# Swapped projections in place of the exchange between partitions, for the first half of the first head pair of each batch

## The reference

```python
q = (xn @ q_w + q_b).reshape(b, s, H, HD).transpose(0, 2, 1, 3)
k = (xn @ k_w + k_b).reshape(b, s, H, HD).transpose(0, 2, 1, 3)
v = (xn @ v_w + v_b).reshape(b, s, H, HD).transpose(0, 2, 1, 3)
# _rope(x): x1, x2 = x[..., 0::2], x[..., 1::2]
#   concatenate([x1 * cos - x2 * sin, x1 * sin + x2 * cos], axis=-1)
q, k = _rope(q, theta), _rope(k, theta)
scores = jnp.einsum('bhqd,bhkd->bhqk', q, k) * scale   # causal softmax follows
```

## Time and profile before

| | us |
|---|---|
| median of 3 runs (2248.17 to 2252.59) | 2251.11 |
| the profiled execution | 2248.88 |
| its span, first to last instruction | 2247.1 |
| TensorE busy | 1943.8 (87%) |
| VectorE busy | 1620.2 (72%) |
| ScalarE busy | 1459.2 (65%) |
| GpSimd busy | 948.8 (42%) |

### The profile page before, as it was taken

How to read it: one execution, slowest core, us unless ns; L and a number is a source line. 1 busy time by engine, 2 the same in 40 slices (tenths; PEclk the granted TensorE clock), 3 DMA queues, 4 the chain that set the end, 5 groups by cost and what they waited for, 6 DMA issues and landing times. The chain is left out here.

```text
span 2247.1 us, 33201 instructions
## 1 busy us (share of the span) xinstructions
PE 1943.8 (87%) x10218; PEld 1300.2 (58%) x10218; DVE 1620.2 (72%) x3001; ACT 1459.2 (65%) x2909; POOL 948.8 (42%) x909
## 2 busy tenths in 40 slices
PE   3759999889985999988988699998898679999798
PEld 1236676657524767665742567676574256676566
DVE  4867777658696777766768777775777877776587
ACT  2528777657652878765765477775675367777576
POOL 2555353234365443413436635341443564352243
PEclk9879999989987999998989799999998989999899
DMA  2001111001101111100110111110010011010011
GB/s 80 1 21 43 28 37 32 8 22 41 38 0 34 30 39 26 39 10 20 41 31 0 43 29 37 33 28 15 22 40 15 1 42 43 22 41 20 20 35 33
DMA packets 63328, 64.09 MB, mean 29 GB/s; under 512 B 12104, under 2 KB 46256, under 8 KB 63152
## 3 DMA queue, kind: packets, MB, share of 16 engines
q1 hardware_dynamic: 63152, 61.96, 10.5%
HBM read 26.26 MB, written 2.10 MB: 13 GB/s over the span
## 5 line engine op out<-in xcount | busy, mean ns | idle before, releaser
L787 ACT ACTIVATE probs<-ps,least 128x640 f32<-128x640 f32 (+7 forms) x512 | 380.6, 743 | 85.9 <-DVE least L1134 74.6
L799 ACT ACTIVATE probsT<-ps 128x512 f32<-128x512 f32 (+3 forms) x768 | 348.4, 491 | 120.3 <-PE ps L1504 111.9
L1504 PE MATMUL ps<-ident,probs 128*128 128x128 f32 x2304 | 349.2, 277 | 11.8 <-ACT probsT L799 4.5
L1494 PE MATMUL ps<-k_high,q_split 128*128 128x512 f32 (+3 forms) x768 | 303.6, 395 | 54.5 <-DVE q_split L1124 37.0
L1504 PEld LDWEIGHTS ps<-ident,probs 128*128 128x128 f32 x2304 | 271.3, 141 | 51.8 <-issue 22.6
L509 POOL TENSOR_SCALAR inverse_wide<-inverse 128x512 f32<-128x512 f32 x64 | 39.7, 621 | 545.8 <-DVE inverse L1145 545.8
L1141 DVE TENSOR_REDUCE least<-ps 128x1 f32<-128x640 f32 (+3 forms) x256 | 262.2, 1024 | 8.8
L1515 PE MATMUL ps<-probsT,vals 128*64 128x512 f32 (+3 forms) x1408 | 265.4, 498 | 0.4
L1495 PE MATMUL ps<-k_low,q_split 128*128 128x512 f32 (+3 forms) x768 | 261.5, 353 | 0.0
L1494 PEld LDWEIGHTS ps<-k_high,q_split 128*128 128x128 f32 x768 | 147.9, 193 | 177.6 <-ACT probs L787 85.7
L870 ACT ACTIVATE hid<-ps,cols 128x512 f32<-128x512 f32 x256 | 176.3, 689 | 112.6 <-PE ps L1341 112.2
(11 more groups left out here) (222 smaller groups left out, 3996.3 us busy)
## 6 DMA issues: line engine op xcount, KB each, us to landing
roped<-turned SPq DMA_DIRECT2D x512, 64.0 KB, 2.0
w<-in_w SPq DMA_DIRECT2D x128, 128.0 KB, 2.0
w_pair<-in_w_pairs SPq DMA_DIRECT2D x32, 128.0 KB, 2.6
xin<-in_x SPq DMA_DIRECT2D x4, 512.0 KB, 4.3
out<-acc SPq DMA_DIRECT2D x4, 512.0 KB, 3.2
pos<-in_c_pos SPq DMA_DIRECT2D x1, 512.0 KB, 4.7
v_w<-in_v_w SPq DMA_DIRECT2D x1, 512.0 KB
o_w<-in_o_w SPq DMA_DIRECT2D x1, 512.0 KB
```

The costliest lines, as they stand in the source:

```text
L787: act.activation(probs[:, t % 2, 0:width(t)], banks(2 * (t % 2))[:, 0:width(t)], ACT.Exp, bias=least[:, t:t + 1], scale=-1.0, accum_out=ro ...
L799: act.activation(dst, ps[:, T_BANK + g % 2, 0:k1 - k0], ACT.Copy).then_inc(t_taken, 1)
L1494: pe.matmul(o, q, k_high[par][h][:, k0:k1], start=True, stop=False)
L1504: made = pe.transpose(ps[:, T_BANK + g % 2, at - k0:at - k0 + P], probs[:, t % 2, at:at + P], ident[:, :])
```

## The change

For the first half of the first pair of each batch, the swapped sine part is computed and not fetched. A second weight tensor `w_sw` (columns in swapped order, one DMA at the start, split into high and low parts by GpSimd once) gives the projection with its partitions already exchanged, in banks 2 and 3. VectorE multiplies it by sin and subtracts it from the cosine part, in place of the exchange and GpSimd's addition. On GpSimd `acc` stands behind the preparation of both halves. On TensorE the values stand behind the scores of units 0 and 1, and on VectorE the order of the second half's products, the minima and the values changes. The second half and all other pairs keep the exchange.

```diff
@@ program: buffers, semaphores
+SW_BANK = (2, 3)
+        w_sw = sb("w_sw", [P, 2, P])
+        w_sw_high, w_sw_low = sb("w_sw_high", [P, 2, P], F32R), sb("w_sw_low", [P, 2, P], F32R)
...
@@ sync
+            sp.dma_start(w_sw[:, :, :], ins["w_pairs"][0:1, :, 1::2, :].rearrange("o p s n -> p (o s) n")).then_inc(w_sw_in, 16)
             part_end(sp, 1)
...
-                    for c in range(HALVES):
+                    for c in range(HALVES) if p else (1,):
@@ gpsimd, once, before the batches
+            pool.wait_ge(w_sw_in, 16)
+            pool_copy(pool, w_sw_high[:, :, :], w_sw[:, :, :]).then_inc(w_sw_split, 1)
+            pool.wait_ge(w_sw_split, 1)
+            pool.tensor_tensor(w_sw_low[:, :, :], w_sw[:, :, :], w_sw_high[:, :, :].bitcast(F32), ALU.subtract
+                               ).then_inc(w_sw_split, 1)
+            pool.wait_ge(w_sw_split, 2)
@@ gpsimd, prepare
                     def add(j):
-                        pool.wait_ge(swapped[j], DMA_ALL * (m + 1))
+                        if (p, c) == (0, 0):
+                            pool.wait_ge(roped_ready, 2 * m + j + 1 + 2)
+                            return
+                        pool.wait_ge(swapped[j], DMA_ALL * (m - b))
@@ gpsimd, each batch
                 pool.wait_ge(xn_split, 2 * b + 2)
+                for c in range(HALVES):
+                    prepare(0, 0, c, lambda k: k, lambda: None)
                 pool.wait_ge(y_stored, 16 * b + 16)
                 pool.wait_ge(tok_ready, 2 * b + 2)
                 steps.link(pool.tensor_tensor(acc[:, :, :], xa[:, :, :], gamma1_r.unsqueeze(1).broadcast_to((P, TILES, P)),
                                               ALU.mult))
                 pool.tensor_tensor(acc[:, :, :], acc[:, :, :], o_b_r.unsqueeze(1).broadcast_to((P, TILES, P)),
                                    ALU.add).then_inc(acc_ready, 1)
-                for c in range(HALVES):
-                    prepare(0, 0, c, lambda k: k, lambda: None)
@@ vector
-                for g in range(4):
-                    sine(b * PAIRS, 0, g, g, PROLOGUE_BANK[g])
-                    cosine(0, g, PROLOGUE_BANK[g])
+                for j in range(2):
+                    m = HALVES * b * PAIRS
+                    dve.wait_ge(x_out, X_ALL * b + j + 1)
+                    dve.wait_ge(roped_ready, 2 * m + j + 1)
+                    cosine(0, j, PROLOGUE_BANK[j])
+                    dve.wait_ge(sw_out, 2 * b + j + 1)
+                    dve.scalar_tensor_tensor(roped[:, j, cols_of(0)], ps[:, SW_BANK[j], :], cols[:, C_QK + 2 * (1 - j) + 1:
+                                             C_QK + 2 * (1 - j) + 2], sin_t[:, cols_of(0)], ALU.add, ALU.mult
+                                             ).then_inc(sine_ready, 1)
+                    dve.wait_ge(x_taken, X_ALL * b + j + 1)
+                    dve.wait_ge(sine_ready, 2 * m + j + 1)
+                    dve.sem_inc(passed, 1)
+                    dve.tensor_tensor(roped[:, j, cols_of(0)], turned[:, 0, j, :], roped[:, j, cols_of(0)], ALU.subtract
+                                      ).then_inc(roped_ready, 1)
+                sine(b * PAIRS, 0, 2, 2, PROLOGUE_BANK[2])
                 for h in range(2):
                     low(b * PAIRS, 0, 0, h)
+                sine(b * PAIRS, 0, 3, 3, PROLOGUE_BANK[3])
+                smallest(b * PAIRS, 0)
+                cosine(0, 2, PROLOGUE_BANK[2])
+                cosine(0, 3, PROLOGUE_BANK[3])
+                smallest(b * PAIRS, 1)
                 for c in range(2):
                     values(0, 0, 4 + c, c, PROLOGUE_BANK[c])
-                for t in range(2):
-                    smallest(b * PAIRS, t)
@@ tensor
                     project(g, 0, PROLOGUE_BANK[g])
+                    if g < 2:
+                        if (b, g) == (0, 0):
+                            pe.wait_ge(w_sw_split, 2)
+                        parts_product(ps[:, SW_BANK[g], :], w_sw_high[:, 1 - g, :], w_sw_low[:, 1 - g, :], cut(xn_high, 0),
+                                      cut(xn_low, 0), True, True).then_inc(sw_out, 1)
+                for t in range(2):
+                    scores(b * PAIRS, 0, t)
                 for c in range(2):
                     bank_free(c + 1)
                     values(0, c, PROLOGUE_BANK[c])
-                for t in range(2):
-                    scores(b * PAIRS, 0, t)
```

More of the change, by code:

```diff
@@ L326, in program @@
         w_pair_high_ready, w_pair_split = sem("w_pair_high_ready"), sem("w_pair_split")
+        w_sw_in, w_sw_split, sw_out = sem("w_sw_in"), sem("w_sw_split"), sem("sw_out")
         x_out, x_taken = sem("x_out"), sem("x_taken")
```

## The result

The changed kernel takes 2255.47 us in the median of 20 runs (2251.34 to 2260.53), the kernel before 2249.26 in 20 runs beside them. The ratio is 1.0028 with a 95% interval of 1.0018 to 1.0038: 6.3 us slower, 4.0 to 8.5. The profiled executions are nearer together: 2252.60 against 2248.88, spans 2250.8 against 2247.1. One execution of experiment 4, 3599 us at a lower clock, was disturbed and is left out of its ratio; all others are counted.

What follows compares the result with a forecast made beforehand. Bound: each batch's opening, a latency chain with GpSimd in it. Late third sine products, 3 x 0.5 + 1.0 = +2.5 us, on the profiled 2248.88 give 2251.4, median 2253.6, said as 2253.5; range 2244 to 2260.

Steps and rivals of the forecast that it cites:

- the gate: Pair 1's third sine product on VectorE waits for GpSimd's fifth addition: 0.5 us late, 1.0 in fourth batch, +2.5 in all.
- Keys, queries, low parts: Batch 0's opening: keys 152.5, queries 155.05, low parts 158.8, scores 159.0, first exponential 160.1, 5.4 us early.
- The mutual exclusion: Low parts: two-input operations of VectorE and GpSimd follow one another; mere sharing would make the sum about 4 us smaller.
- Values in the path: Values behind the first scores on TensorE put pair 1's projection at 163.55, leaving 1.8 of 5.4 us.
- rival B: All 5.4 us of the earlier first exponential stay, needing the values hidden too: 2229.5 us; chance 0.03.
- the alternative of the text: With the clock at its upper level from 163.5 on, GpSimd's fifth addition would end at about 174.5.
- My own case: The forecast sum with pair 1's third sine product late, +2.5 us; own range 2246.5 to 2257.6; chance 0.58.
- rival C: TensorE's clock low after VectorE's stall: +1.1 to +2.2 us per batch, +7 to +11 in all, about 2260; chance 0.20.
- the sign that the prediction set for C: Third sine product at 174.7, but the step ends over 1 us later, with granted clock 0.5 after the stall.
- C's last sentence: Decisive is whether the stall's gap at TensorE matches its idle stretch when the clock fell; stall computed near 3 us.
- A: GpSimd gets through `acc` sooner or VectorE arrives later, so the 1.8 us stay: -7.2 us, 2244; chance 0.13.
- D: VectorE's subtraction waits for GpSimd's copies, shrinking the head start by a further us; same time as forecast; no separate chance.

Runs made afterwards that it cites:

- experiment 4: Kernel before with only the `acc` operations moved late, behind GpSimd's part of the first step: 2248.98 us, ratio 1.0010.
- Experiment 6: Changed kernel with `acc` back at its old place, ahead of pair 0's preparation: 2251.12 us, ratio 1.0003 against the kernel before.
- experiment 1: Changed kernel with `acc` moved later still, behind GpSimd's part of the first step: 2243.23 us, ratio 0.9969 against the kernel before.
- experiment 3: Changed kernel with `acc` behind GpSimd's part of the first step and the values ahead of the first scores: 2239.64 us, ratio 0.9952 against the kernel before.
- experiment 2: Changed kernel with the values back ahead of the first scores on TensorE: 2253.83 us, ratio 1.0023 against the kernel before.
- experiment 7: Kernel before with only the `acc` operations moved behind pair 0's preparation: 2265.80 us, ratio 1.0075.
- experiment 5: Changed kernel with fifteen unread products on TensorE in each first step's stall: 2256.47 us, ratio 1.0028 against the kernel before.
- experiment 8: Experiment 5 with VectorE's first two low parts one unit later: 2251.22 us. Its line, from six kernels: rest of step is 20.74 to 20.77 plus unit 7's low part.

## Why the prediction was right, and where it wasn't

The forecast was 2253.5, the measurement 2255.47, inside the range, and part of that is luck. The forecast was +2.4 us on a median of 3 runs, 2251.11; 20 runs of the kernel before gave 2249.26, and the measured change is +6.3. Against the profiled execution, to which the sum was made, the forecast was +2.5 and the marks give +4.67, with the gate booked too high, the clock not at all, and a third term that nobody had (the holds, below). By its own steps, in batch 0's times:

*Keys, queries, low parts.* Keys 152.59 (forecast 152.5), queries 154.73 (155.05), low parts done 158.36 (158.8), scores 158.57 (159.0), first exponential 159.57 (160.1). The mutual exclusion on which the low parts' time rested is there: GpSimd's two operations take 2.93 us together, VectorE's two take 2.93 us as well, and they end 0.55 apart. Experiment 6 shows it by itself, a subtraction of 2.81 beside `acc` against 0.69. The Trainium skill (SBUF — State Buffer, "SBUF: two separate sides") says the same, as a lock held for the whole instruction, and the rows agree.

*Values in the path.* 163.46 against 163.55: of the first exponential's head start, the six takings leave 1.9 us. Experiments 1 and 3 show that this much is real and is kept where nothing downstream takes it: 2.20 earlier at pair 1's first sine product and 2.16 at the end of the step in experiment 1 (against before), 2.82 and 2.88 in experiment 3. That is also the answer to rival B: 5.74 us of earlier first exponential are worth 2.2.

*The gate.* The fifth addition ended at 173.92, not at 174.5 to 175.0: the clock was at its upper level from 163 on, so GpSimd's second `k_low` did not have to wait, and `acc` started at 167.57 instead of 168.3; this was the alternative of the text, put lower. That VectorE's low part falls into `acc` came out as said (1.34 in batch 0, the second `acc` operation at 2.67), only that in batch 1 it was held 2.90. In sum +1.55 where I had +2.5, and not evenly: I had booked every batch as late, and batches 0 and 2 passed 0.27 and 0.35 earlier than before. Experiments 1, 2, 3 and 7 show that it is this gate and the place of `acc` ahead of it: opening it gives back 13 us, closing it in the kernel before costs 13 (17 by the ratio). Of what the values gained ahead of it, 1.2 of 2.9 us came out while it was closed and all of 2.5 when it was open, by one profiled execution each.

*TensorE's clock, the step that failed.* My own case booked nothing for it, rival C +7 to +11 in all. It is in every batch, and it costs 0.69 us each from the third sine product to the fourth, +2.74. The TensorE timelines show what the 0.69 is. Pair 1's fourth projection in batch 3 of the changed kernel:

```profile
1832.30 0.80 PE L1369 MATMUL ps<-xn_high,w_pair_high 128*128 128x512 f32 x1
...
1833.32 0.63 PE L1371 MATMUL ps<-xn_high,w_pair_low 128*128 128x512 f32 x1
```

and the same projection in experiment 5, batch 0:

```profile
180.76 0.50 PE L1369 MATMUL ps<-xn_high,w_pair_high 128*128 128x512 f32 x1 [0.70 <-DVE turned L1116]
...
181.33 0.39 PE L1371 MATMUL ps<-xn_high,w_pair_low 128*128 128x512 f32 x1
```

From start to end it is 1.65 us at the lower level and 0.96 at the upper. The difference, 0.69, is all that this stretch takes longer: in batch 2, where the scores ahead of the projection still ran at the upper level, the term is 0.67 as well.

Behind the fourth product the clock stayed down for another 1.1, 2.1, 4.4 and 1.2 us, and the line of experiment 8 gives an estimate of what that cost. The rest of the step less the duration of the low part (0.69 in all four) is 21.27, 21.39, 21.46 and 21.25, where the 24 batches at the upper level have 20.74 to 20.77: 0.50 to 0.71 us more, 2.4 in all. The eight batches of experiments 2 and 7, in which the clock was down too, have 21.19 to 21.40. A missing backlog behind the stall isn't the reason, since experiment 5 has the same stall and lies on the line of the others. So the clock costs some 5.1 us in all, 1.2 to 1.4 a batch by this estimate, and that is within the 1.1 to 2.2 that C had named. The mechanism was C's, and so, as far as is shown, was the price of a batch; By the sign that the prediction set for C, a step that ends over 1 us later, it is met in batches 1 and 3 (2.06 and 1.32) and not in batches 0 and 2 (0.49 and 0.80). C's total was too high because it stood on +2.5 of the gate, and because of the holds, which no rival had.

The reasoning error is in C's last sentence: I set VectorE's stall, near 3 us, against the idle stretch of TensorE before the clock fell in the kernel before (from 154.7, still 1.00 in the window 158 to 159, 0.51 in the next). What had to be compared was TensorE's own gap, which starts with its last transposes at 170.93 and ends only when the sine product, the minimum and the exponential have followed the stall, 4.26 us. The step counted only VectorE's part of it. Even so the comparison would have been a draw, 4.26 against the 4.3 us that the idle stretch of the kernel before had lasted when the clock fell. The second half of the error is to take that length for a condition. The fall came sooner than there: about 2 us into the idle time in batches 0, 1 and 3, and after the gap in batch 2. Experiment 5 shows that the gap causes it: with products in it the clock stays up and 2.74 us come back.

*The rest.* +0.38. This is the clock's 2.4 against 2.0 of holds that went away: VectorE's low part of unit 7 took 1.15, 0.91, 0.91 and 1.76 in the four batches before and takes 0.69 in all of them in the changed kernel. So the three terms of the profile are +1.55, +2.74 and +0.38. That filling the stall did not move the time, though the clock term was gone, is shown by experiments 5 and 8: a faster TensorE brought VectorE's low part under GpSimd's addition. The line gives the +1.93 of experiment 5 as 4.3 of holds less 2.4 of clock.

*Rivals.* A (the gate does not close) fails by 2.95 us of idle time. D (the subtraction waits for GpSimd's copies) cost nothing, but the rows don't refute its mechanism. The second subtraction took 0.69 beside a copy of which only 0.15 us was left. Launched at the start of such a copy, a two-input operation of VectorE is held by it too, as these rows of the changed kernel, from the step of a later pair, show:

```profile
289.04 0.61 POOL L515 TENSOR_SCALAR k_high<-roped 64x512 fp32r<-64x512 f32 x1 [0.20 <-POOL roped L613]
289.07 1.13 DVE L1139 SCALAR_TENSOR_TENSOR q_split<-roped,q_split 64x512 fp32r<-64x512 f32 x1
```

The slower outcome had 0.25, "within 0.2%" had 0.57; the measured 0.28% lies just beyond. Had the clock been in the sum, the slower outcome would have had the larger chance.

*Open.* The ratio says 6.3 us (4.0 to 8.5), the marks 4.7, the profiled executions 3.7. The distance from one batch's start to the next varies by 3.7 us in the profile before (552.38, 552.06, 548.64) and by 1.5 after (550.57, 552.03, 551.82). The difference is inside that, and no run here ties it to a part of the change. The marks of each kernel come from one profiled execution, and the clock ahead of the gate moves the third sine product of a batch by more than 1 us (experiment 1), so a difference of 1 or 2 us between two sums isn't a finding by itself.

## What to carry to other kernels

Follow a head start past the place where it arises, to the next wait of another engine that does not move with it: here a filler block moved out of the cleared stretch landed just ahead of such a wait, cost 13 us, and hid a gain of 8 to 9. At its old place it would have taken that gain as well. Before an engine's gap is called harmless, work out the gap of TensorE itself, from its last product to its next, and not the stall of the engine that it waits for. Put filler work of GpSimd where it crosses neither a gate nor a two-input operation of VectorE that others wait for, and test a part that was moved "to make room" by itself on the kernel before.

## What the runs showed of the hardware that was not expected

- A VectorE operation with two SBUF inputs (the low parts and subtractions here) that is launched while a GpSimd operation runs ends 0.53 to 0.55 us behind the end of that one, whatever it is. In the changed kernel it is so in all 26 cases in which more than 0.2 us of GpSimd's operation was left, behind `acc`, additions, `k_low` and one-input copies alike. So 0.69 us becomes 1.77 when launched 0.05 behind an addition of 1.27 (experiment 5), 0.91 when launched 0.90 behind one (kernel before, batch 1), and stays 0.69 when launched 1.14 behind it (experiment 8).
- It works the other way round too. GpSimd's copy, 0.61 when alone, ends 0.48 behind the VectorE operation during which it was launched, an addition of 1.27 ends 1.12 to 1.15 behind it (1.74 in all in experiment 1), and the second `acc` operation of 2.37 ends 2.20 behind it (2.67 in all).
- Such a hold goes one to one into a step whose chain runs through VectorE (24 batches, experiment 8), and a speed-up of another engine can trigger it: the same low part took 0.69 in the changed kernel, where the clock was lower, and 1.77 where it wasn't. One unit's delay avoids it.
- The granted clock fell about 2 us into an idle stretch of TensorE in three batches of the changed kernel, and in batch 2 about 1 us behind a gap of 4.16. In the openings of batch 0 it fell 4.3 us into the idle stretch in the kernel before, and 4.8 us after the last product, with TensorE already at work for 0.6, in the changed kernel. The fifteen products in the stall kept it at 1.00.
